# Summing whole squares with one fp32 product for all heads, and an earlier projection in the first batches of a decoder kernel

## The reference, cut to what matters

```python
# self-attention, per batch
q, k, v = x @ w_q.T, x @ w_k.T, x @ w_v.T            # 16 heads of 32
attn = softmax(where(causal, q @ k.T / sqrt(32), -inf))
x = layernorm(x + (attn @ v) @ w_o.T)
# queries of the cross-attention, per head of 128
q = x @ Wq + bq
q = q * rsqrt(mean(q * q, axis=-1) + 1e-6) * qn_w
```

## Time and profile before

| | us |
|---|---|
| median of 3 runs | 1592.82 |
| lowest, highest | 1590.75, 1600.2 |
| profiled execution | 1589.74 |
| its span (first to last instruction) | 1587.9 |
| busy in the span: PE, DVE, ACT, POOL | 1436.6, 893.7, 751.7, 673.0 |
| mean granted clock of PE | 0.967 |

### The profile page before, as it was taken

The page is one execution under the profiler, slowest core; times in us unless marked ns, Lnnn a source line. Parts: engine busy times, 40 slices in busy tenths (PEclk is TensorE's granted clock), DMA queues, the critical chain, the costliest instruction groups (busy, mean ns, idle before and its releaser), DMA issues. The chain is left out here.

```text
span 1587.9 us, 25327 instructions
## 1 busy us (share of the span) xinstructions
PE 1436.6 (90%) x8553; PEld 1212.6 (76%) x8553; DVE 893.7 (56%) x3074; ACT 751.7 (47%) x1981; POOL 673.0 (42%) x1000
## 2 busy tenths in 40 slices
PE   7789999899876789999999999999999999399976
PEld 7568878788765578888888888888888888277854
DVE  3534555545555575557655665556655674743347
ACT  4536575666734353444444444444434445243246
POOL 1214354444544274343444444444443444264164
PEclk9989999999988999999999999999999999699988
DMA  5201232231333342211121111112122113475363
GB/s 188 84 14 55 79 94 74 64 114 53 104 122 107 126 123 71 61 56 55 43 71 51 62 59 43 61 56 65 36 68 61 56 42 111 150 234 164 111 206 120
DMA packets 86423, 139.60 MB, mean 88 GB/s; under 512 B 11323, under 2 KB 54687, under 8 KB 85400
## 3 DMA queue, kind: packets, MB, share of 16 engines
q1 hardware_dynamic: 81720, 123.04, 24.3%
q0 software_dynamic: 4576, 14.95, 3.3%
HBM read 93.50 MB, written 44.46 MB: 87 GB/s over the span
## 5 line engine op out<-in xcount | busy, mean ns | idle before, releaser
L1394 POOL TENSOR_TENSOR b_pcarry<-b_half 128x1 f32<-128x1 f32 x173 | 47.1, 272 | 382.5 <-DVE b_rinv L1264 344.2
L1152 ACT ACTIVATE b_probs<-b_probs,b_nmax 100x361 f32<-100x361 f32 x256 | 152.0, 594 | 72.8 <-DVE b_nmax L1258 72.4
L74 PE MATMUL bank<-b_kTh,b_q 128*100 128x362 f32 x512 | 171.2, 336 | 6.4 <-issue 4.8
L1258 DVE CUSTOM_DVE_ANT_0 b_probs<-bank,b_mask 100x361 f32<-100x361 f32 x256 | 135.6, 530 | 50.4 <-issue 42.1
L1419 POOL TENSOR_SCALAR b_probs<-b_probs,b_rinv 100x361 f32<-100x361 f32 x256 | 162.4, 646 | 0.0
L1193 ACT ACTIVATE b_oTh<-bank,b_bv 128x400 fp32r<-128x400 f32 x64 | 38.0, 594 | 222.6 <-PE bank L74 222.6
L1147 ACT ACTIVATE b_pTh<-bank 121x400 fp32r<-121x400 f32 x192 | 96.5, 503 | 92.8 <-PE bank L984 88.0
L1251 DVE TENSOR_TENSOR b_pTl<-bank,b_pTh 121x400 fp32r<-121x400 f32 x192 | 109.8, 572 | 52.5 <-ACT b_pTh L1147 52.4
L984 PE MATMUL bank<-ident,b_probs 100*121 100x100 f32 x768 | 109.7, 265 | 4.6 <-POOL b_probs L1419 3.3
L984 PEld LDWEIGHTS bank<-ident,b_probs 100*121 100x121 f32 x768 | 107.0, 185 | 7.2 <-POOL b_probs L1419 4.5
L74 PE MATMUL bank<-b_Woh,b_oTh 128*100 128x512 f32 x256 | 110.7, 432 | 1.4 <-DVE b_oTl L1322 1.4
(11 more groups left out here) (259 smaller groups left out, 4060.4 us busy)
## 6 DMA issues: line engine op xcount, KB each, us to landing
q_d<-a_qo SPq DMA_DIRECT2D x128, 200.0 KB, 2.4
b_q<-q_d SPq DMA_DIRECT2D x64, 400.0 KB, 3.2
b_ctxr<-in_ctxT SPq DMA_DIRECT2D x48, 242.0 KB, 4.0
y_d<-c_y SPq DMA_DIRECT2D x32, 256.0 KB
c_Eraw<-in_expert_w SPq DMA_DIRECT2D x10, 512.0 KB, 7.7
a_stage<-in_Wq SPq DMA_DIRECT2D x4, 1024.0 KB
stage<-in_Wo SPq DMA_DIRECT2D x8, 512.0 KB, 4.8
a_xTr<-in_xT SPq DMA_DIRECT2D x8, 400.0 KB
```

What stands on the lines that cost most here:

```text
L74: mm = eng.matmul(out, lhsT=l(c), rhs=r(c), start=first and k == 0, stop=last and k == n - 1)
L1152: act.activation(p, p, ACT.Exp, scale=-1.0, bias=nmax[:, s % 2, h:h + 1], accum_out=psums[:, s % 2, h:h + 1]).then_inc(e_rdy, 1)
L1258: dve.tensor_tensor_reduce(out=probs[:, s % 2, h, 0:SE], in0=s_bank[h % 2][0:S, 0:SE], in1=mask_s[:], scale=-1.0, scalar=BIG, op0=ALU.add, ...
L1394: pool.tensor_tensor(pcarry[:, k:k + 1], half_s[:, 0:1], half_s[:, 0:1], ALU.add)
```

## The change

Part 1, all heads: ACT squares `qb` once, in fp32, into `qsq`, which has two buffers (`head_squares`), and PE sums it by a single product with ones in fp32. POOL's square and DVE's subtraction are gone. In the tail ACT's order is logarithm and exponential of head m - 1, then the square of head m. The weight pieces and the third context tile move to later heads.

Part 2, batches 0 to 3: the projection for the next pair stands right behind the value product, in banks 4 and 5 (`p_bank`), which the heads use only from batch 4 on. In batches 1 to 4 the transposes of x1 stand behind the value product.

```diff
-KV_FRAME, CTX_FRAME = (50, 52, 56, 58), (48, 50, 55)
+KV_FRAME, CTX_FRAME = (50, 52, 59, 61), (48, 50, 57)
...
+        def p_bank(pair, is_q, half):
+
+            return bank[4 + half] if 1 <= pair <= GB // 2 else bank[half if is_q else 2 + half]
...
             def square_sums(m):
                 if m == 0:
                     pe.wait_ge(ones_set, 1)
-                pe.wait_ge(sq_hi, m + 1)
+                pe.wait_ge(sq_set, m + 1)
                 if m >= TAIL + 2:
                     pe.wait_ge(ln_set, m - 1)
-                pe.wait_ge(sq_lo, m + 1)
-                pe.matmul(ss_bank(m)[:, 0:GT], lhsT=ones_r[:], rhs=qsh[:], start=True, stop=False)
-                pe.matmul(ss_bank(m)[:, 0:GT], lhsT=ones_r[:], rhs=qsl[:], start=False, stop=True).then_inc(ss_done, 1)
+                pe.matmul(ss_bank(m)[:, 0:GT], lhsT=ones_s[:], rhs=qsq[:, m % 2], start=True, stop=True).then_inc(ss_done, 1)
...
-                if i >= 1:
+                if i > GB:
                     transpose_x1(i - 1)
                 product3(pe, bank[7][0:S, :], lambda c: xTh[:, c, cols], lambda c: xTl[:, c, cols],
                          lambda c: wvh[:, c, :], lambda c: wvl[:, c, :], range(2, DC), first=False).then_inc(v_done, 1)
+                if 1 <= i <= GB:
+                    transpose_x1(i - 1)
+                if i < GB:
+                    project(pair + 1, (wk_s, wq_s)[par], range(DC), (wk_in, wq_in)[par])
...
-                if pair + 1 < NPAIR:
+                if i >= GB and pair + 1 < NPAIR:
                     if par == 0:
                         project(pair + 1, wk_s, range(DC), wk_in)
...
-            def squares_hi(m):
+            def head_squares(m):
                 if m is None:
                     return
                 act.wait_ge(q_ev, m + 1)
-                wait(act, ss_done, m)
-                act.activation(qsh[:], qb[:, m % 2], ACT.Square).then_inc(sq_hi, 1)
+                wait(act, ss_done, m - 1)
+                act.activation(qsq[:, m % 2], qb[:, m % 2], ACT.Square).then_inc(sq_set, 1)
...
             for m in range(t + 1, NQ):
-                squares_hi(m)
                 root_log(m - 1)
                 root_exp(m - 1)
+                head_squares(m)
...
-            def squares_lo(m):
-                if m is None:
-                    return
-                dve.wait_ge(sq_hi, m + 1)
-                dve.wait_ge(sq_set, m + 1)
-                dve.tensor_tensor(qsl[:], qsq[:], qsh[:].bitcast(F32), ALU.subtract).then_inc(sq_lo, 1)
...
-            def squares(m):
-                if m is None:
-                    return
-                wait(pool, ss_done, m)
-                pool.wait_ge(q_ev, m + 1)
-                pool.tensor_tensor(qsq[:], qb[:, m % 2], qb[:, m % 2], ALU.mult).then_inc(sq_set, 1)
```

More of the change, by code:

```diff
@@ L154, in self_attention_phase @@
         qrs, qn = sb("a_qrs", [P, 2, GT]), sb("a_qn", [P, 2, GT])
-        qb, qsh, qsq, qsl, ones_r = qwork
+        qb, qsq, ones_s = qwork
         bank = head.bank
@@ L172, in self_attention_phase @@
         x1T_done, x1T_hi, x1T_lo = sem("x1T_done"), sem("x1T_hi"), sem("x1T_lo")
[L173 removed]
+        qx_done, q_ev, sq_set = sem("qx_done"), sem("q_ev"), sem("sq_set")
         ss_done, ln_set, qrs_set, q_rdy, q_hi, q_lo = sem("ss_done"), sem("ln_set"), sem("qrs_set"), sem("q_rdy"), sem("q_hi"), sem("q_lo")
@@ L271, in project @@
                     for c in range(DC):
-                        mm = pe.matmul(bank[m // 2 if is_q else 2 + m // 2][:, m % 2 * 2 * S:(m % 2 + 1) * 2 * S],
+                        mm = pe.matmul(p_bank(pair, is_q, m // 2)[:, m % 2 * 2 * S:(m % 2 + 1) * 2 * S],
                                        lhsT=w[:, c, m * P:(m + 1) * P], rhs=xTr[:, c, :], start=c == 0, stop=c == DC - 1)
@@ L408, in scaled_q @@
                 act.wait_ge(qs_done, 2 * pair + half + 1)
-                act.activation(qTs[:, 2 * half:2 * half + 2].rearrange("p c t -> p (c t)"), bank[half][:, 0:4 * S], ACT.Copy,
+                act.activation(qTs[:, 2 * half:2 * half + 2].rearrange("p c t -> p (c t)"), p_bank(pair, True, half)[:, 0:4 * S], ACT.Copy,
                                scale=float(SHD) ** -0.5).then_inc(qs_ev, 1)
@@ L486, in _ @@
                     rows_hi(i - 1)
-                squares_hi(m[0])
+                head_squares(m[0])
                 queries_hi(before - 1)
@@ L497, in _ @@
                 probs_T(i, 1)
-                squares_hi(m[1])
+                head_squares(m[1])
                 root_exp(m[0])
@@ L504, in _ @@
                 queries_hi(before)
-                squares_hi(m[2])
+                head_squares(m[2])
                 act.wait_ge(oT_done, i + 1)
@@ L518, in _ @@
                 queries_hi(m[1])
-                squares_hi(m[3])
+                head_squares(m[3])
                 root_log(m[2])
@@ L525, in _ @@
             queries_hi(t - 2)
-            squares_hi(t)
+            head_squares(t)
             queries_hi(t - 1)
@@ L556, in copy_k @@
                 dve.tensor_copy(kTn[:, 2 * half:2 * half + 2].rearrange("p c t -> p (c t)"),
-                                bank[2 + half][:, 0:4 * S]).then_inc(kn_ev, 1)
+                                p_bank(pair, False, half)[:, 0:4 * S]).then_inc(kn_ev, 1)
             def split_xT(pair):
@@ L633, in _ @@
             dve.tensor_scalar(qkw_s[:, 3:4], qkw_s[:, 2:3], float(XHD) ** 0.5, None, ALU.mult).then_inc(qkw_set, 1)
-            dve.tensor_scalar(ones_r[:], ident_s[:], 0.0, 1.0, ALU.mult, ALU.add).then_inc(ones_set, 1)
+            dve.memset(ones_s[:], 1.0).then_inc(ones_set, 1)
             split_lo(0)
@@ L755, in _ @@
                 normalise(i, 1)
-                squares(m[0])
                 queries_lo(before - 1)
@@ L759, in _ @@
                 normalise(i, 3)
-                squares(m[1])
                 if par == 1 and pair + 1 < NPAIR:
@@ L764, in _ @@
                 queries_lo(before)
-                squares(m[2])
                 queries_lo(m[0])
                 queries_lo(m[1])
-                squares(m[3])
             t = TAIL
@@ L771, in _ @@
             queries_lo(t - 2)
-            squares(t)
             queries_lo(t - 1)
@@ L776, in _ @@
                     split_context(CTX_FRAME.index(m - 1))
-                squares(m)
                 if m >= t + 2:
@@ L2066, in build @@
         a = args
-        with nc.sbuf_tensor("a_qb", [P, 2, GT], F32) as qb, nc.sbuf_tensor("a_qsh", [P, GT], F32R) as qsh, \
-                nc.sbuf_tensor("a_ones", [P, P], F32R) as ones_r:
-            with nc.sbuf_tensor("a_qsq", [P, GT], F32) as qsq:
-                pass
-            with nc.sbuf_tensor("a_qsl", [P, GT], F32R) as qsl:
-                pass
+        with nc.sbuf_tensor("a_qb", [P, 2, GT], F32) as qb, nc.sbuf_tensor("a_qsq", [P, 2, GT], F32) as qsq, \
+                nc.sbuf_tensor("a_ones", [P, P], F32) as ones_s:
+            pass
         stage = ctx.enter_context(nc.sbuf_tensor("stage", [P, 2, 2, D], F32))
```

8 lines of the change are left out of this document (1 added, 7 removed).

## The result

| us | before | changed |
|---|---|---|
| median, beside each other (4 runs each) | 1592.23 (1590.75 to 1600.2) | 1547.52 (1546.59 to 1548.65) |
| profiled execution, its span | 1589.74, 1587.9 | 1547.77, 1545.8 |
| mean granted clock of PE | 0.967 | 0.978 |
| busy: PE, DVE, ACT, POOL | 1436.6, 893.7, 751.7, 673.0 | 1433.7, 849.7, 753.5, 615.5 |

The ratio is 0.971, 95% interval 0.9677 to 0.9743. A second measurement, on another chip, gave 1538.24 against 1579.79: 0.9745 (0.9728 to 0.9761).

The account below looks back on a forecast made before the run. PE was taken to bound batches 4 to 15, and a chain over three engines the tail. Tail -32, batches 4 to 15 +4, batches 0 to 3 -5 gave -33: 1556.7, plus 3.1 for the median, 1560 us; own range 1550 to 1571.

Parts of the forecast that it names:

- batches 4 to 15: PE-bound batches: 46 dearer sums +15.2, less low-half waits 8.8 and `xTr` waits 3.4, plus 1: +4 us, bounds +15 and -5.
- wider range: Whole kernel: 1545 to 1581 us, the range with rivals A, C and D included.
- Rival A: Tail: third and fourth weight pieces come late at heads 59 and 61; tail -23, total -24, 1570 us; chance 0.14.
- C: Square sums: the fp32 product costs 0.96 to 1.03 us like the slow projection; total -14, 1579 us; chance 0.05.
- D: Batches 0 to 3: the projection does not fill PE's softmax wait; early part 0, total -28, 1565 us; chance 0.07.
- The tail: Heads 48 to 63: 16 heads of 2.88 us plus 4.5 late, 50.6 against 82.9: -32 us, between -24 and -37.
- the three operations of ACT fit beside PE: Tail: ACT's log, exponential and square take 1.70 us plus some 0.2 signalling, within PE's 2.18; 0.3 us to spare.
- The price of the sum: All heads: one fp32 product at 0.70 us replaces two fp32r products at 0.364, +0.33 per head where PE is bound.
- upper bound of 1.03: Square sum: dearest fp32 product, at half clock throughout like the 7.65 us projection (0.96), and a little for weights.
- waits for `xTr`: Batches 4 to 15: the store ahead of the load comes 0.85 us earlier, four waits shrink by 0.85 each, -3.4 us.
- Batches 0 to 3: Early projection and moved x1 transposes: +3, -4.6, +1, -4 us by batch, sum -5; bounds +3 and -10.
- Rival B: Tail and batches: the waits were never the low half's, tail pays 5.3 more; total +23.5, 1616 us; chance 0.04.

Follow-up runs that it names:

- experiment 5: Changed kernel with ACT's old order in the tail, square of head m ahead of logarithm and exponential of head m-1: ratio 0.978 to the kernel before, tail 56.3 us.
- experiment 4: Changed kernel with weight pieces and third context tile back at old heads (56, 58 and 55): ratio 0.9801 to the kernel before, tail 62.3 us.
- part 2 alone: Kernel before with only the early projection and moved x1 transposes, squares still summed by two fp32r products: ratio 0.9941 to the kernel before, front 509.3 us.

## Why the prediction was right, and which step was off

1560 was forecast and 1547.52 measured. Of the 12.5 us between them 9.1 lie in the profiled executions (-33 forecast, -42.1 found); 3.1 were added because the median before lay above the profiled execution, which it did not in the changed kernel (1547.52 beside 1547.77). Of the 9.1 us 7.0 are the step "batches 4 to 15". That the time still lies in the wider range is no merit of its lower end: rivals A, C and D all make the kernel slower than forecast, and none of them gives 1545.

- **The tail, -32 forecast, -32.4 found.** The loop through POOL's square and DVE's low half set the tail; without it PE does, at 2.85 us a head (forecast 2.88). 16 x 2.85 are 45.6 us, and the four waits, shown as 3.9 us, make up the other 4.9, where 4.5 were summed: 2.75 shown at the context tile with the first weight piece (forecast 1 and 0.7 to 1.2), 0.39 to 0.40 at each of the other pieces. The sentence that the three operations of ACT fit beside PE came to the right result by the wrong reason: they fit because of the new order, which experiment 5 shows to be worth 5.9 us.
- **The price of the sum, 0.70 forecast, 0.67 found.** The row of the projection, scaled by columns, was the right one to take. By the Trainium skill, "FP8 and Floating Point Precision", section TensorE Precision Notes, it would be 0.73, an estimate from its four passes; the measured product is 0.67 / 0.182 = 3.7 times the fp32r one. The upper bound of 1.03 was called half clock and is not: at a granted clock of 0.50 the sum of experiment 4 has a record of 1.70 us instead of 0.83.
- **Batches 4 to 15, +4 forecast, -3.0 found: the step that failed.** The sum comes to +0.6 for a batch with four sums, and it holds where nothing else changed: batches 5, 7, 9, 11 and 13 are 0.62 to 0.65 longer. With 0.85 off for `xTr` it comes to -0.2, and batches 8 and 12 are 0.3 shorter. It fails in batches 6 and 10 (-2.0 and -3.0) and in 14 and 15 (-0.3 and -1.0). Term by term:

| term | forecast | found | difference |
|---|---|---|---|
| price of 46 sums | 0.33 each | 0.30 each | -1.4 |
| waits for `xTr` | -3.4 | -4.8, 2.0 of them in batch 10 | -1.4 |
| waits on ACT's root (`a_qrs`, batches 14 and 15), x1 and `x1Tl` | 0 | 3.1 to 1.4, 2.3 to 1.8 | -2.2 |
| clock behind the waits for `xTr`, batches 6 (181.54) and 10 | 0 | projection 7.36 to 5.68, twice | -3.4 |
| wait for the probabilities | +1 | +5.6 shown, +5.0 from start to start | +4.0 |
| 11 waits for the low half | -8.8 | -11.5 from start to start | -2.7 |

Together that is -7.1, the whole of the 7.0 within rounding. The last row is read from lines like these, of batch 7 before:

```profile
202.80 0.34 PE L74 MATMUL bank<-a_x1Th,a_Wql 128*128 128x400 f32 x1
204.03 0.42 PE L297 MATMUL bank<-a_qsh,a_ones 128*128 128x400 f32 x1 [0.89 <-DVE a_qsl L613]
204.29 0.35 PE L298 MATMUL bank<-a_qsl,a_ones 128*128 128x400 f32 x1
204.47 1.79 PE L354 MATMUL bank<-ident,a_probs 100*100 100x100 f32 x16
```

From the last query product to the transposes these are 1.67 us, where three products without a wait take 3 x 0.182 = 0.55: a wait shown as 0.89 cost 1.12. Over the 11 batches the same stretch took 17.5 us, 6.0 without waits. In the changed kernel it is 0.85 or 0.86 in each. Why the projection of batch 6 ran slow before is open: part 2 alone has the same wait (1.91 us) and full clock.

- **Batches 0 to 3, -5 forecast, -5.4 found,** with the right sign in each batch, but not by the right terms in each. Batch 0 lost 4.2 (forecast +3). Its output product starts at 43.37, behind a wait of 3.62 us for `oTl`; counted from the first scores that is 2.0 us later than before, not 3. The other 2.1 are the product itself, which takes 5.1 us instead of 3.0, with 0.50 of the clock granted from 43.4 to 47.7; the sum did not hold this. Batch 1 gained 6.6 and batch 3 5.4, more than forecast by 2.0 and 1.4. PE's busy time fell by 3.4 and 3.5 us, where the clock was priced at 2.1 and 1.2, because not only the projection had been slow (the heads' product of batch 1 went from 1.56 to 0.89 us). Its idle time fell by 3.2 and 1.9, where 2.5 and 2.8 were forecast. Batch 2 lost 2.4, not 1: the wait for `xTr` was 4.57 us (4.8 forecast), but the projection behind it took 7.36 us, where the sum counted on 1 us back from the clock.
- **Rival A** (pieces late at heads 59 and 61) did not come, but experiment 4 shows its mechanism at the old heads, with a cost of 11.8 us in the tail. **Rival B**: the tail did not stay at 4.49, but an order on ACT does make a loop, at 3.10. **C** fell with the price of 0.67, **D** with the gains of batches 1 and 3.
- The rule of the Trainium skill, "GPSIMD Engine Reference", section Key points, that POOL contends with DVE instructions of two SBUF inputs, is seen: the scaling takes 1.41 us beside POOL's subtraction (444.83 above) where it is 0.64 elsewhere. It stands in the chain that ends in the wait of 2.75 us, so some 0.8 us of that may be its price; no run takes it out. At the other three pieces the wait is 0.39 us each, so the 0.8 us more for each piece did not come.

## What to carry to other kernels

When a stage is bound by a loop over several engines, write the loop down with every in-order neighbour, not only the operations that depend on each other; the order of three short operations on ACT was worth 5.9 us here and moved no load on any engine. When a wait of several us in front of PE's work goes, or comes, price also the low clock of what stands behind it: it was 1.7 us on a 5.6 us projection behind the waits of 3.0 and 4.6 us here, and 2.1 us on the output product of batch 0 behind 3.6 us. Price a short wait by the starts of the instructions around it, not by the idle time shown. And when a stage gets faster, move its supplies too (weight pieces, the load of `xTr`): these gave 10.9 and 11.8 us of the front, each more than part 2 alone (7.6).

## What the runs showed of the hardware

- A projection of 5.6 us took 7.4 us behind waits of 3.03 us (294.30 in the kernel before) and 4.57 us (75.19 above), with 0.50 of full speed granted in part of it, and 6.7 to 7.8 us in batches 1 to 3 of the kernel before, where PE had stood idle several times (58.72 is one). Near 1.9 us the length of the wait does not decide: in the kernel before 1.87 us (181.54) was followed by 7.36 us, but 1.92 and 2.04 in batches 12 and 8 by 5.7, and 1.91 in batch 6 of part 2 alone by 5.68 too. With waits of at most 1.1 us for `xTr` in batches 4 to 15 the granted clock stayed at 1.00, full speed (2.4 GHz).
- A wait of PE shown as 0.86 to 0.93 us ahead of a square sum cost 1.10 to 1.17 us from start to start, and one shown as 0.36 cost 0.6.
- The same program behind the first value product of the next stage took 1039.7 to 1053.5 us, by chip and run. A front of 475.9 us repeated to 0.1 us on two chips.
- A loop that holds PE back by 0.25 us a head leaves no wait on PE in the profile; it shows in the pace from start to start, and in a record of 0.94 instead of 0.83 us.
